# Macaron block with a mixture of experts: the begin of the first dispatch written out to tile 7, memory cleared by VectorE, weights split two a batch

## The reference

```python
x = x + 0.5 * ffn(layernorm(x))
x = x + attention(layernorm(x))          # phi = silu + 1, kv = phi_k^T v, out = phi_q kv, then Wo
x = x + 0.5 * ffn(layernorm(x))

def ffn(x):
    shared = (silu(x @ gate) * (x @ up)) @ down
    probs = sigmoid(x @ router + bias)   # 8 experts
    scores, indices = top_k(probs, 2);  scores /= sum(scores)
    return shared + sum over the 2 picked experts e of score_e * (silu(x @ gate_e) * (x @ up_e)) @ down_e
```

## Time and profile before

| | |
|---|---|
| median of 3 runs | 775.2 us (774.94 to 776.71) |
| the profiled execution, by its own time | 777.83 us |
| its span, first to last instruction | 776.1 us |
| busy: TensorE, VectorE, ScalarE, GpSimd | 89%, 71%, 60%, 70% |
| chain that ended last: TensorE, VectorE, DMA, GpSimd | 61%, 13%, 4%, 3% |
| mean granted clock of TensorE | 0.94 of 2.4 GHz |

### The profile page before, as it was taken

The page is one execution under the profiler, slowest core; times in us unless marked ns, Lnnn a source line. Parts: engine busy times, 40 slices in busy tenths (PEclk is TensorE's granted clock), DMA queues, the critical chain, the costliest instruction groups (busy, mean ns, idle before and its releaser), DMA issues.

```text
span 776.1 us, 17587 instructions
## 1 busy us (share of the span) xinstructions
PE 688.4 (89%) x4981; PEld 612.8 (79%) x4981; DVE 550.5 (71%) x1842; ACT 469.2 (60%) x865; POOL 539.5 (70%) x569
## 2 busy tenths in 40 slices
PE   5586967969999969999899999999989999999980
PEld 4475766859999969998667777777669999999980
DVE  6686877886555538886679987787787555577772
ACT  3335534525766747686777676766547767777750
POOL 3474777777777777777447676767777777777772
PEclk8588867999999989999999999999999999999995
DMA  9313221143354346554203111111333453567765
GB/s 280 97 52 121 76 65 52 53 121 109 103 161 136 100 118 188 173 179 120 79 27 100 43 42 46 43 42 46 88 101 103 130 163 105 159 188 222 222 195 169
DMA packets 63445, 89.65 MB, mean 116 GB/s; under 512 B 13174, under 2 KB 43768, under 8 KB 63352
## 3 DMA queue, kind: packets, MB, share of 16 engines
q1 hardware_dynamic: 46456, 53.63, 24.6%
q0 software_dynamic: 16896, 34.90, 13.3%
HBM read 46.36 MB, written 42.12 MB: 114 GB/s over the span
## 4 chain that ended last, share of the span: by engine, by line
PE 61%; DVE 13%; DMA 4%; issue 4%; POOL 3%; ACT 1%; SPq 1%; POOLq 0%; DVEq 0%; ACTq 0%
PE y_bank L1119 13%; PE g_bank L921 4%; PE y_bank L1013 4%; PE u_bank L923 4%; PE u_bank L922 4%; PE u_bank L921 4%; PE g_bank L923 4%; PE g_bank L922 4%; PE g_bank L992 3%; PE u_bank L993 2%; POOL x_rows L633 2%; PE route_bank L1073 2%; PE y_bank L1196 2%; DMA send<-x_rows 2%; PE tr_bank L943 2%
## 5 line engine op out<-in xcount | busy, mean ns | idle before, releaser
L633 POOL DMA_INDIRECT x_rows<-send,send_to x256 | 248.9, 972 | 129.5 <-issue 72.5
L645 POOL DMA_INDIRECT y_rows<-send,y_to x272 | 266.5, 980 | 84.6 <-issue 68.4
L1778 DVE TENSOR_TENSOR h<-silu_g,u_bank 128x512 f32<-128x512 f32 x136 | 93.4, 687 | 115.3 <-ACT silu_g L822 109.7
L797 ACT ACTIVATE slot_gu<-w_gu 128x1024 fp32r x130 | 137.7, 1059 | 38.8 <-issue 35.6
L1119 PE MATMUL y_bank<-w_dn,h 128*128 x1088 | 144.4, 276 | 0.8 <-DVE x L1339 0.4
L1119 PEld LDWEIGHTS y_bank<-w_dn,h 128*128 128x128 f32 x1088 | 133.7, 192 | 1.2 <-issue 1.2
L921 PE MATMUL g_bank<-xT_hi,slot_gu 128*128 128x256 f32 x260 | 85.2, 328 | 9.4 <-DVE xT_lo L1769 8.3
L1013 PEld LDWEIGHTS y_bank<-w_dn,h 128*128 128x128 f32 x512 | 65.5, 203 | 26.7 <-issue 26.0
L822 ACT ACTIVATE silu_g<-g_bank 128x512 f32<-128x512 f32 x136 | 79.0, 581 | 8.8 <-PE g_bank L923 8.5
L1013 PE MATMUL y_bank<-w_dn,h 128*128 128x128 f32 x512 | 67.1, 287 | 16.3 <-DVE x L1339 16.3
L696 ACT ACTIVATE silu_g<-g_bank 128x512 f32<-128x512 f32 x64 | 38.0, 597 | 67.8 <-PE u_bank L923 42.4
(11 more groups left out here) (258 smaller groups left out, 1478.1 us busy)
## 6 DMA issues: line engine op xcount, KB each, us to landing
send<-x_rows SPq DMA_DIRECT2D x130, 130.0 KB
y_pair<-y_rows SPq DMA_DIRECT2D x32, 512.0 KB
y_rows<-send,y_to POOLq DMA_INDIRECT x272
x<-x_in SPq DMA_DIRECT2D x16, 256.0 KB, 7.3
x_rows<-send,send_to POOLq DMA_INDIRECT x256
out<-x SPq DMA_DIRECT2D x16, 256.0 KB
w_raw<-w_experts SPq DMA_DIRECT2D x15, 256.0 KB, 3.5
x_rows<-pad SPq DMA_DIRECT2D x16, 130.0 KB, 2.3
```

Of the source, the lines that this page charges most:

```text
L633: pool.indirect_dma_start(x_rows, bass.IndirectOffsetOnAxis(ap=send_to[b % SEND_TO_RING][:, w, k:k + 1], axis=0), send[ring_of(f, t)][:, w ...
L645: pool.indirect_dma_start(y_rows, bass.IndirectOffsetOnAxis(ap=y_to[k][:, j:j + 1], axis=0), result_rows(f, s)[:, j, :], None).then_inc(y_ ...
L797: act.activation(slot_gu[n % 2][:].rearrange("p a n -> p (a n)"), w_gu[:, bass.ds(e, 1)].rearrange("p e a n -> p (e a n)").bitcast(F32), A ...
L1778: dve.tensor_tensor(h[par][0][:], silu_g[par][:], u_bank[par][:], ALU.mult).then_inc(slot_h_done, 1)
```

## The change

It does five things, all in the first dispatch.

1. GpSimd clears nothing of the five tiles any more. VectorE clears four of them before its first `norm`, and `pad` behind the first part of `route` of batch 1.
2. The written-out part goes to tile 7 (`WRITTEN_OUT = 4`, four batches and the look-ahead to batch 4), in a new order on three engines: `ranks` of batches 2 and 3 stand in front of shared experts, ScalarE normalises and transposes ahead of `silu_tile`, and VectorE routes batches 2 and 3 before it multiplies for the shared expert. In the loop `multiply_tile` of a batch's first tile stands always in front of the second part of `route`.
3. Tiles 8 to 11 are normalised in two calls, (8, 9) and (10, 11), instead of one.
4. The weights: experts 1 and 2 are split at the end of the written-out part, and 3 to 8 two a batch in batches 4 to 6. Before it was 1 to 3 there, then 4 and 5, 6 and 7, and 8.
5. The first matrix multiplications that only warm TensorE up are 15 instead of 18.

```diff
-    calls = [... ((0,), (1,), (2, 3), (4, 5), (6, 7), (8, 9, 10, 11), (12, 13, 14, 15))]
+    calls = [... ((0,), (1,), (2, 3), (4, 5), (6, 7), (8, 9), (10, 11), (12, 13, 14, 15))]
...
-WARM_UP = 18
-WRITTEN_OUT = 3
+WARM_UP = 15
+WRITTEN_OUT = 4
+SPLIT_IN = {4: (3, 4), 5: (5, 6), 6: (7, 8)}
... GpSimd
-            pool.memset(nobody_pad, 0.0).then_inc(pool_cleared, 1)
-            pool.memset(pad[:], 0.0).then_inc(pool_cleared, 1)
-            pool.memset(passed[:], 0.0).then_inc(pool_cleared, 1)
-            pool.memset(single[:], 0.0).then_inc(pool_cleared, 1)
-            pool.memset(cell_value[:], 0.0).then_inc(pool_cleared, 1)
... TensorE, dispatch
+                ranks(f, 2)
                 gate_up_tile(f, 1)
-                ranks(f, 2)
                 down_shared(f, 0)
+                transpose_x((FFN, f, 4))
+                router(f, 4)
+                transpose_x((FFN, f, 5))
+                router(f, 5)
                 gate_up_tile(f, 2)
                 down_shared(f, 1)
-                transpose_x((FFN, f, 4))
+                ranks(f, 3)
                 gate_up_tile(f, 3)
-                router(f, 4)
-                transpose_x((FFN, f, 5))
                 down_shared(f, 2)
-                router(f, 5)
+                transpose_x((FFN, f, 6))
+                gate_up_tile(f, 4)
+                router(f, 6)
+                transpose_x((FFN, f, 7))
+                down_shared(f, 3)
+                router(f, 7)
+                gate_up_tile(f, 5)
+                down_shared(f, 4)
... VectorE, dispatch
                 route(f, 1, 0, MASK_STEP)
+                dve.memset(pad[:], 0.0).then_inc(cleared, 1)
                 low((FFN, f, 2))
...
-                multiply_tile(f, 0)
                 route(f, 2, 0, ROUTE_STEPS)
                 row_tails(f, 2)
+                multiply_tile(f, 0)
+                norm(3)
                 multiply_tile(f, 1)
-                norm(3)
                 add_shared(f, 0)
+                low((FFN, f, 4))
+                low((FFN, f, 5))
+                route(f, 3, 0, ROUTE_STEPS)
+                row_tails(f, 3)
                 multiply_tile(f, 2)
+                add_shared(f, 1)
                 norm(4)
-                add_shared(f, 1)
-                low((FFN, f, 4))
                 multiply_tile(f, 3)
-                low((FFN, f, 5))
+                add_shared(f, 2)
+                low((FFN, f, 6))
+                multiply_tile(f, 4)
+                low((FFN, f, 7))
+                add_shared(f, 3)
+                norm(5)
+                multiply_tile(f, 5)
+                add_shared(f, 4)
                 padding_constants()
-                add_shared(f, 2)
-                for t in range(1, 4):
-                    split_low(t)
+                for e in range(1, 3):
+                    split_low(e)
... VectorE, first instructions
+            dve.memset(nobody_pad, 0.0)
+            dve.memset(passed[:], 0.0)
+            dve.memset(single[:], 0.0)
+            dve.memset(cell_value[:], 0.0).then_inc(cleared, 1)
```

More of the change, by code:

```diff
@@ L52, in norm_calls @@
 def norm_calls():
-    calls = [[(FFN, 0, t) for t in ts] for ts in ((0,), (1,), (2, 3), (4, 5), (6, 7), (8, 9, 10, 11), (12, 13, 14, 15))]
+    calls = [[(FFN, 0, t) for t in ts] for ts in ((0,), (1,), (2, 3), (4, 5), (6, 7), (8, 9), (10, 11), (12, 13, 14, 15))]
     groups = [[(ATTN, 1, t) for t in range(t0, t0 + 4)] for t0 in range(0, TILES, 4)]
@@ L295, in macaron @@
         memsets, consts_ready, counted, pad_ready = sem("memsets"), sem("consts_ready"), sem("counted"), sem("pad_ready")
-        counting_ready, cleared, pool_cleared = sem("counting_ready"), sem("cleared"), sem("pool_cleared")
+        counting_ready, cleared = sem("counting_ready"), sem("cleared")
         split_hi, split_lo = sem("split_hi"), sem("split_lo")
@@ L740, in dispatch @@
                 route_silu(f, 0)
-                silu_tile(f, 0)
                 send_normalised(f, 2)
@@ L746, in dispatch @@
                 high((FFN, f, 3))
+                silu_tile(f, 0)
                 send_second(f, 2)
                 send_second(f, 3)
+                route_silu(f, 2)
                 silu_tile(f, 1)
-                route_silu(f, 2)
-                split_high(1)
-                silu_tile(f, 2)
                 send_normalised(f, 4)
@@ L755, in dispatch @@
                 send_normalised(f, 5)
-                silu_tile(f, 3)
-                send_normalised(f, 6)
                 high((FFN, f, 5))
-                send_normalised(f, 7)
+                split_high(1)
                 send_second(f, 4)
                 send_second(f, 5)
-                split_high(2)
-                split_high(3)
+                silu_tile(f, 2)
+                route_silu(f, 3)
+                send_normalised(f, 6)
+                silu_tile(f, 3)
+                high((FFN, f, 6))
+                send_normalised(f, 7)
+                silu_tile(f, 4)
+                high((FFN, f, 7))
                 send_second(f, 6)
                 send_second(f, 7)
+                silu_tile(f, 5)
+                normalise_batch(f, 5)
+                split_high(2)
                 for b in range(WRITTEN_OUT, len(BATCHES[f])):
@@ L778, in dispatch @@
                             silu(f * tiles + ts[1], c)
+                    for e in SPLIT_IN.get(b, ()):
+                        split_high(e)
                     for t in ts:
-                        if 1 <= t < EXPERTS:
-                            split_high(t)
                         if t == tiles - 3:
@@ L1727, in dispatch @@
                         low((FFN, f, ahead[0]))
-                    if b > WRITTEN_OUT:
-                        multiply_tile(f, ts[0])
+                    multiply_tile(f, ts[0])
                     route(f, b, MASK_STEP, ROUTE_STEPS)
                     row_tails(f, b)
-                    if b == WRITTEN_OUT:
-                        multiply_tile(f, ts[0])
                     if ts[0] == COUNTED:
@@ L1865, in constants @@
                 dve.wait_ge(counting_ready, 1)
-                dve.wait_ge(cleared, 1)
+                dve.wait_ge(cleared, 2)
                 dve.tensor_copy(number_weight[:, :, :, 0], part(counting, 0).rearrange("p (w n) -> p w n", w=PICKS)
@@ L1874, in padding_constants @@
             def padding_constants():
-                dve.wait_ge(pool_cleared, 5)
+                dve.wait_ge(cleared, 3)
                 unused = nobody_numbers.rearrange("p (b j) -> p b j", j=JS)
```

## The result

| | before | after |
|---|---|---|
| median | 775.2 us | 783.0 us (782.05 to 785.5, 4 runs) |
| profiled execution (span) | 777.83 us (776.1) | 782.05 us (780.3) |
| ratio of the runs, with its 95% interval | | 1.0081 (1.0052 to 1.011): 6.3 us (4.0 to 8.5) |
| GpSimd begins batch 3, batch 4, batch 5, tile 10 | 77.48, 98.16, 119.48, 140.21 us | 67.10, 99.71, 124.10, 144.63 us |
| the middle's first work on GpSimd | 376.43 us | 380.58 us |

The change makes the kernel 0.8% slower. The forecast was 780.4 us, in a range of 773.5 to 785.5 us, which holds the result.

A forecast was written before the change was run, and what follows sets the result against it. The prediction took GpSimd's queue of sends as the bound from 77 to 376 us. Tile 10's 5.2 us delay, with nothing from fewer warm-up matmuls, was added to the 775.2 us median: 780.4 us, range 773.5 to 785.5 us.

The forecast's parts named there:

- The bound, GpSimd's queue: From 77 to 376 us GpSimd's indirect sends, 1.27 us apart, set the pace; a microsecond lost there is lost at the end.
- Theory 2, the start of the slot stage: Experiments' rival: VectorE's and TensorE's end of the dispatch costs, the queue has slack; queue delay 0 to 1 us.
- Part 1: Kernel's head: VectorE clears memory, `half_var` falls 3.75 us, batch 0's tails come at 19.0 instead of 22.39 us.
- the prediction's other price for it: Clearing `pad` on VectorE at one cycle per element: 2.2 us, making the sum 0.3 us worse.
- Batch 3 earlier, batch 4 not: GpSimd starts batch 3 10.8 us earlier, then waits 12.4 us before batch 4, which starts 1.6 us later.
- The rival in which the front's gain survives: Batch 4's tails at 91 us, tile 10 sent 2.3 us sooner, kernel faster at 772.9 us; chance 0.17.
- Batches 5 to 8: Second `norm` call delays batch 5's tails to 124.0 us; GpSimd waits some 5 us, tile 10 goes 5.2 us later.
- the rival with TensorE at 1.2 GHz in front of batch 4: Shared experts before batch 4 run at half clock, adding 4 to 7 us: 784 to 788 us; chance 0.15.
- The end of the tiles' sends: In the first dispatch, GpSimd sends without a gap until about 239 us, after VectorE ends the routing.
- The sum: Whole kernel: +5.2 us, tile 10's delay in the queue, on the median of 775.2 us, giving 780.4 us.

The follow-up runs named there:

- the first experiment: The kernel before, with GpSimd's send of tile 12 made to wait for the last batch's row tails: 780.56 against 776.02 us, ratio 1.0071.
- the second experiment: The kernel before with seven VectorE memsets behind the last batch's row tails: ratios 0.9997 and 1.0005, both on chips where before took some 989 us.
- memory and late splits: The kernel before with VectorE clearing memory and experts 1 to 8 split two a batch in batches 4 to 7: 769.49 against 776.02 us.
- the change, late splits: The changed kernel with experts 1 to 8 split two a batch in batches 4 to 7: 780.17 against before's 776.47 us, ratio 1.0063.

## Why the prediction was right, and where it was off

- **The bound, GpSimd's queue:** right, shown by the first experiment and by the table. Theory 2, the start of the slot stage, is refuted by the first experiment as the thing that sets the middle; whether a much later start would cost something was not settled, as the second experiment ran only on the disturbed kind of chip.
- **Part 1:** `half_var` at 0.37 us (0.2 forecast), batch 0's tails at 18.98 us (19.0), the four memsets together 2.1 us (2.0), `pad` 1.79 us (1.83; the prediction's other price for it, 2.2 us, does not hold). The block of 3.95 us is longer than any one memset of GpSimd, so the prediction was too quick to find it in agreement with a block for one instruction; the last section has what the traces show.
- **Batch 3 earlier, batch 4 not:** tails at 66.16 and 98.77 us (65.7, 98.5). The work between them was 25.8 us (25.3), the waits 6.8 us (7.7), in the places that were forecast: 3.5 us at the multiplies, 2.2 at the split of expert 2, 0.6 at a low part, 0.5 at an addition (3.8, 2.3, 0.8, 0.8). The wait in front of batch 4 is 12.57 us (12.4). The rival in which the front's gain survives needed the tail before 93.3 us. The start of batch 4 before was 98.16 us and not 97.9; the loss there is 1.55 us (1.6).
- **Batches 5 to 8:** tails at 123.16 us (124.0) and at the end 169.60 us (170.6), the wait in front of batch 5 4.35 us (5), tile 10 at 144.63 us (145.4), the slot stage's first low part 4.9 us later (5 to 6), the middle at 380.58 us (near 382). The mis-sized term is the stretch between the tails of batches 4 and 5: 24.4 us instead of 25.5. The second call of `norm` itself took 3.4 us (3.5), but a wait of 0.8 us of VectorE for ScalarE's SiLU that stood there before is gone.
- **The clock:** the rival with TensorE at 1.2 GHz in front of batch 4 did not come: the granted clock from 66 to 99 us was 0.90, before it had been 0.86 from 77 to 97 us. It did fall earlier: from 30 to 66 us it was 0.67, before 0.81, and batch 3's tails came 0.5 us later than forecast. The three matmuls less at the start were not tried alone.
- **The end of the tiles' sends** was put at 239 us; the last one begins at 204.84 us, and before it was 200.07 us. No other number rests on it.
- **The sum:** +5.2 us from the trace of before. By the two profiled executions it is +4.2 us (782.05 less 777.83), so the sum was 1 us too high, and the stretch above is most of it. By all runs the change costs 6.3 us (4.0 to 8.5), by the medians alone 7.8 us; +5.2 us lies in that interval.
- **What the sum was added to** is the weak step: a difference of traces was put on a median. The profiled execution of before was a long one. Against it, every later kernel looks better than by its runs:

| kernel, against before | by the profiled executions | by the medians on the same chip |
|---|---|---|
| the change | +4.2 us | +7.8 us |
| queue late at tile 12 | +1.9 us | +4.5 us |
| memory and late splits | -10.6 us | -6.5 us |
| the change, late splits | +1.7 us | +3.7 us |

The differences are 2.0 to 4.1 us. The 780.4 us lie 2.6 us under the measured median for this reason and not for a wrong wait, and that they lie inside a range of 12 us is little proof of them.

Why before's profiled execution was long is open. One candidate is the head: in that execution GpSimd's memsets block VectorE for 3.95 us; in the trace of the queue experiment, whose head is that of before, they do so for far less:

```profile
4.46 0.17 DVE L1284 TENSOR_SCALAR half_var<-stats 128x4 f32<-128x4 f32 x1
4.66 1.54 DVE L1286 TENSOR_SCALAR guess<-half_var 128x4 int32<-128x4 int32 x1
...
19.30 0.18 DVE L1448 COPY send<-number_weight 128x16 f32<-128x16 f32 x1 [0.52 <-DVE number_weight L1437]
```

and GpSimd's memsets in it:

```profile
4.55 1.63 POOL L610 MEMSET y_pair<- 128x1820 f32 x1
6.12 1.85 POOL L611 MEMSET pad<- 128x2080 f32 x1
```

The first small step is free here, the second takes 1.54 us and ends at 6.20 us, with GpSimd's memset of `y_pair` (4.55 + 1.63 = 6.18 us), batch 0's tails are at 19.30 us instead of 22.39, and tile 10 goes out 2.4 us sooner than in the earlier trace rows. The profiled execution of before stood 2.6 us above its median, so a short block in most executions would account for it. Against that, of the five traces with before's memsets only this one has it (three of the others are of the disturbed kind of chip, with 3.44, 3.97 and 3.47 us).

The other candidate is the clock. On the two usual chips, eight runs of before with a mean granted clock of 0.938 to 0.941 average 777.5 us, sixteen with 0.942 and more 775.4 us; the profiled execution has 0.940 and took 777.83 us. And kernels whose GpSimd clears nothing scatter as well: the change with late splits took 779.1 to 780.8 us in five runs at 0.940 and more, and 782.7 to 783.9 us in three at 0.936 to 0.938. Which of the two it was, and whether the clock is a cause or goes along with something else, no run here tells.

## What to carry to other kernels

When one queue is the bound, write down when each batch reaches it, and move a batch forward only if the next one follows: 10.4 us won for batch 3 became a gap, because what was taken from in front of it was put in front of batch 4. What helped, by 3.15 us at tile 10 in the one pair that differs in nothing else, was to put off work that nobody waits for (the expert weights) until the queue was ahead. And before a gain is set against a median, look whether the profiled execution is one of the ordinary ones.

## What the runs showed of the hardware

How long GpSimd's memsets hold up VectorE is not one number. With the same instructions, VectorE's four-column steps were blocked for 3.95, 3.97, 3.47 and 3.44 us in `half_var`, and once for 1.54 us in the step behind it. Each block ends with a memset of GpSimd: at 8.48 us with the last of five, twice (the traces with 3.95 and 3.97 us); at 7.95 and 7.96 us with the second, `pad`; at 6.20 us with the first, in the fence above. So VectorE goes on after one, two or five memsets. Where `half_var` was free it had begun at 4.46 us; where it was blocked, at 4.48 to 4.53 us, and GpSimd's first memset is recorded from 4.54 to 4.56 us on. A few hundredths of a microsecond in the landing of x lie between the two cases.

The Trainium skill (page "SBUF — State Buffer", section "Who interferes with whom") says that whoever issues first has the shared port pair for its whole instruction, and that the order of issue decides who blocks. The traces agree that VectorE stands still, and show that several instructions of GpSimd can follow each other in one block: `pad`'s memset of 1.83 us is only a part of the 3.95 us.

Taking the five memsets away leaves a small block: in the change `half_var` takes 0.37 us instead of 0.17. In the five traces without them in which it begins before 4.35 us, it ends at 4.63 to 4.64 us whatever its length (0.30 to 0.40 us), and GpSimd's last instruction of its own setup, an `affine_select` on `head_mask` (from 4.21 us, 0.40 us long), ends at 4.61 us. In the other four it begins at 4.47 us or later and takes 0.17 us.

A VectorE memset took 0.86 ns a column (1.79 us for 2080 columns, 1.57 us for 1820), about what GpSimd takes (1.83 us for 2080).

GpSimd issued one indirect send each 1.27 us, 0.97 us busy and 0.30 us to the next, and this rate bounded the kernel up to the middle from the first batch on behind which no gap came.

Chips differ: on the three of the disturbed kind the same program took 27% longer at a granted clock of 0.87 to 0.89 instead of 0.94, with VectorE's instructions as long as ever (0.69 us for 512 columns). The time is in waits: GpSimd waits 20.51 and 10.17 us in front of batches 3 and 4 in the rows at the head of the experiments, and the last send of the first dispatch begins at 239.38 us in that trace, at 200.07 us in that of before. Why was not tried.
